# Mixing of the modes in a four-layer network: PE adds the two halves of each product with the identity, DVE sums the rest out of PSUM

## What is computed

```python
x_dht = jnp.fft.fftn(x.astype(jnp.complex64), axes=(2, 3)).real
top = jnp.einsum('bixy,ioxy->boxy', x_dht[:, :, :M1, :M2], weights1)
bot = jnp.einsum('bixy,ioxy->boxy', x_dht[:, :, -M1:, :M2], weights2)
...
y = jnp.fft.ifftn(out_dht.astype(jnp.complex64), axes=(2, 3)).real
```

## Time and profile before

| | |
|---|---|
| median of 3 runs | 3552.61 us (3551.06 to 3553.41) |
| profiled execution | 3554.87 us |
| its span in the trace | 3552.9 us |
| mean granted TensorE clock | 0.906 |
| PE / DVE / ACT / POOL busy | 76% / 79% / 47% / 51% of the span |

### The profile page before, as it was taken

The page is one execution under the profiler, slowest core; times in us unless marked ns, Lnnn a source line. Parts: engine busy times, 40 slices in busy tenths (PEclk is TensorE's granted clock), DMA queues, the critical chain, the costliest instruction groups (busy, mean ns, idle before and its releaser), DMA issues.

```text
span 3552.9 us, 48970 instructions
## 1 busy us (share of the span) xinstructions
PE 2697.3 (76%) x12701; PEld 2090.3 (59%) x12701; DVE 2797.8 (79%) x3703; ACT 1681.9 (47%) x2183; POOL 1816.0 (51%) x1292
## 2 busy tenths in 40 slices
PE   0094588699988439599989457869998853959998
PEld 0054467587746428487765446758774642848776
DVE  8985987688885888588878598768888588858887
ACT  7652145466643115556645214546664311555664
POOL 2003154399940237089990315439994023708998
PEclk9997889899999769799999788989999976979999
DMA  6712000888841100578880200088884110057885
GB/s 243 259 37 89 0 0 28 237 194 197 193 138 43 47 0 0 182 179 196 197 222 12 89 0 0 28 237 195 197 193 137 47 43 0 0 186 179 197 196 123
DMA packets 117444, 421.29 MB, mean 119 GB/s; under 512 B 16805, under 2 KB 30901, under 8 KB 106586
## 3 DMA queue, kind: packets, MB, share of 16 engines
q1 hardware_dynamic: 96390, 376.16, 41.1%
q10 hardware_dynamic: 19332, 38.99, 3.2%
q0 software_dynamic: 1616, 4.90, 0.5%
HBM read 340.43 MB, written 75.26 MB: 117 GB/s over the span
## 4 chain that ended last, share of the span: by engine, by line
PE 57%; DVE 18%; issue 14%; DMA 3%; POOL 3%; ACT 2%; DVEq 1%; ACTq 1%; SPq 0%; POOLq 0%
PE psum L536 25%; PE psum L503 15%; PE psum L412 7%; PE psum L438 3%; DVE img L1065 2%; POOL work L846 2%; PE psum L514 2%; PE psum L424 2%; DVE work L1044 2%; DVE small L886 2%; DVE work L1075 2%; DVE small L887 1%; DMA workr<-mx_dram 1%; DVE work L1058 1%; DVE work L1224 1%
## 5 line engine op out<-in xcount | busy, mean ns | idle before, releaser
L846 POOL TENSOR_TENSOR work<-work 128x512 f32<-128x512 f32 x960 | 1276.6, 1335 | 474.2 <-DVE work L1233 369.2
L536 PE MATMUL psum<-workr,w 128*128 128x512 f32 (+1 forms) x5760 | 1364.4, 397 | 122.3 <-DMA workr<-mx_dram 109.6
L536 PEld LDWEIGHTS psum<-workr,w 128*128 128x128 f32 (+1 forms) x5760 | 1088.8, 190 | 397.2 <-issue 110.5
L1224 DVE SCALAR_TENSOR_TENSOR work<-psum,work 128x512 f32<-128x512 f32 x1152 | 741.0, 679 | 69.5 <-PE psum L536 52.3
L824 POOL TENSOR_TENSOR work<-img 128x520 f32 x256 | 388.0, 1547 | 605.5 <-DVE img L1065 327.9
L503 PE MATMUL psum<-workr 128*128 128x512 f32 x2304 | 549.7, 401 | 43.5 <-DVE workr L1132 43.5
L503 PEld LDWEIGHTS psum<-workr 128*128 128x128 f32 x2304 | 438.7, 191 | 157.6 <-issue 48.3
L814 POOL TENSOR_TENSOR work<-work 128x1024 f32<-128x1024 f32 x40 | 112.5, 2841 | 503.3 <-DVE work L1033 498.9
L412 PE MATMUL psum<-work,taps 128*128 x1152 | 260.0, 389 | 53.9 <-DVE work L991 53.9
L696 ACT CAST workr<-psum 128x650 fp32r<-128x650 f32 x128 | 90.0, 703 | 445.6 <-DVE psum L1200 233.6
L1197 DVE TENSOR_TENSOR psum<-psum,work 128x650 f32<-128x650 f32 x128 | 107.9, 843 | 228.6 <-ACT psum L689 228.5
(11 more groups left out here) (184 smaller groups left out, 3519.2 us busy)
## 6 DMA issues: line engine op xcount, KB each, us to landing
work<-gn_dram SPq DMA_DIRECT2D x256, 585.0 KB, 11.5
work<-gn_dram SPq DMA_DIRECT2D x256, 146.2 KB, 3.8
work<-gn_dram SPq DMA_DIRECT2D x128, 292.5 KB, 4.8
work<-in_x SPq DMA_DIRECT2D x16, 2048.0 KB, 7.1
img<-in_x SPq DMA_DIRECT2D x32, 1024.0 KB, 11.7
work<-in_mixw SPq DMA_DIRECT2D x64, 512.0 KB, 4.2
out_x<-work ACTq DMA_DIRECT2D x120, 256.0 KB, 6.3
gn_dram<-img SPq DMA_DIRECT2D x24, 1040.0 KB, 21.2
```

What stands on the lines that cost most here:

```text
L536: mm = T.matmul(bank(m % 6), w5[wt][0:kr, P * n:P * n + P], ft[0:kr], start=(i == 0), stop=(i == 4))
L846: G.tensor_tensor(acc_t[v], acc_t[v], pd_t[(9 * v + n) % 6], ALU.add).then_inc(s_acc, 1)
L1224: V.scalar_tensor_tensor(out=tile4(pd_t[m % 6]), in0=tile4(psum[:, m % 6, :]), scalar=0.0, in1=rv[:, q, y0:y0 + RT, x0:x0 + WO], op0=ALU.m ...
```

## The change

PE gets a part in the mixing: for each product it multiplies the identity with the first 512 columns and with the last 512 and lets both add up in one bank of PSUM (banks 2 to 5, in turn). This sums input channels i and i + 16. `s_half16` counts these. DVE's reduction then reads 512 columns of PSUM, with 16 addends a sum, in place of 1024 of SBUF. PE waits for the product, for `spec` to be taken out of its banks (first two places), and from the fifth place on for the reduction four places back (`s_mix`).

The loop of two rounds on DVE is written out over 16 places, and DVE makes its own products up to three places ahead of the place that it reduces. SP issues the second load of a buffer after `s_half16`, not `s_mix`. POOL's program stays.

```diff
--- before.py
+++ after.py
@@ -229,7 +229,8 @@
         s_l1pe, s_l1act, s_l1dve = sem("s_l1pe"), sem("s_l1act"), sem("s_l1dve")
         s_row, s_rowps, s_spec = sem("s_row"), sem("s_rowps"), sem("s_spec")
         s_w = [sem(f"s_mixw{k}") for k in range(8)]
-        s_prodv, s_prod, s_mix, s_dup, s_ost, s_gz = sem("s_prodv"), sem("s_prod"), sem("s_mix"), sem("s_dup"), sem("s_ost"), sem("s_gz")
+        s_prodv, s_prod, s_half16, s_mix, s_dup, s_ost, s_gz = (sem("s_prodv"), sem("s_prod"), sem("s_half16"), sem("s_mix"),
+                                                                sem("s_dup"), sem("s_ost"), sem("s_gz"))
         s_inv, s_inva, s_invd, s_y1, s_x2 = sem("s_inv"), sem("s_inva"), sem("s_invd"), sem("s_y1"), sem("s_x2")
         s_pg, s_filt, s_fdiag, s_fsp, s_fbc, s_taps = (sem("s_pg"), sem("s_filt"), sem("s_fdiag"), sem("s_fsp"),
                                                        sem("s_fbc"), sem("s_taps"))
@@ -317,7 +318,7 @@
                         hold(sp, s_l1pe, b * L1PE + (NT + 10))
                     sp.dma_start(wr[k], mixw[:, 1024 * k:1024 * k + 1024]).then_inc(s_w[k], 16)
                 for n, k in enumerate(WR_DONE):
-                    hold(sp, s_mix, b * 16 + (n + 1))
+                    hold(sp, s_half16, b * 16 + (n + 1))
                     sp.dma_start(wr[k], mixw[:, 1024 * (8 + k):1024 * (9 + k)]).then_inc(s_w[k], 16)
 
                 sp.wait_ge(s_mix, b * 16 + 16)
@@ -454,6 +455,21 @@
                             mm = T.matmul(bank(2 + h), hc[:, m1, s, :], av[:, m1, 16 * h:16 * h + 16, s, :],
                                           start=(m1 + s == 0), stop=(m1 + s == 2))
                     mm.then_inc(s_l1pe, 1)
+
+                pooled = [k for k in range(8) if k not in WR_DVE]
+                for n in range(16):
+                    j, k = n // 8, WR_DONE[n % 8]
+                    if n >= 4:
+                        pe.wait_ge(s_mix, b * 16 + (n - 3))
+                    if n < 2:
+                        pe.wait_ge(s_spec, b + 1)
+                    if k in WR_DVE:
+                        pe.wait_ge(s_prodv, b * 6 + (3 * j + WR_DVE.index(k) + 1))
+                    else:
+                        pe.wait_ge(s_prod, b * 10 + (5 * j + pooled.index(k) + 1))
+                    for h in range(2):
+                        mm = T.matmul(bank(2 + n % 4), cs("ident"), wr[k][:, 512 * h:512 * h + 512], start=(h == 0), stop=(h == 1))
+                    mm.then_inc(s_half16, 1)
 
                 for g in range(16):
                     if g % 8 == 0:
@@ -1032,18 +1048,18 @@
                                          rrow[:, ch].unsqueeze(2).to_broadcast([P, 16, MODES]), ALU.mult))
                 V.tensor_tensor(sp3[:, :, 0], sp3[:, :, 0], rrow[:, C:2 * C], ALU.subtract).then_inc(s_spec, 1)
                 hold(v, s_spec, b + 1)
-                with v.Fori(0, 2) as j:
-                    pooled = [k for k in range(8) if k not in WR_DVE]
-                    for k in WR_DONE:
-                        if k in WR_DVE:
-                            v.wait_ge(s_w[k], b * 32 + j * 16 + 16)
-                            V.tensor_tensor(wr[k], wr[k], spec, ALU.mult).then_inc(s_prodv, 1)
-                            v.wait_ge(s_prodv, b * 6 + j * 3 + (WR_DVE.index(k) + 1))
-                        else:
-                            v.wait_ge(s_prod, b * 10 + j * 5 + (pooled.index(k) + 1))
-                        V.tensor_reduce(mixed[:, ds(j * (8 * MODES) + k * MODES, MODES)],
-                                        wr[k].rearrange("p (i l) -> p l i", l=MODES), AX.X, ALU.add
-                                        ).then_inc(s_mix, 1)
+                own = [(j, k) for j in range(2) for k in WR_DONE if k in WR_DVE]
+                made = 0
+                for n in range(16):
+                    while made < 6 and own[made][0] * 8 + WR_DONE.index(own[made][1]) <= n + 3:
+                        j, k = own[made]
+                        v.wait_ge(s_w[k], b * 32 + (16 * j + 16))
+                        V.tensor_tensor(wr[k], wr[k], spec, ALU.mult).then_inc(s_prodv, 1)
+                        made += 1
+                    v.wait_ge(s_half16, b * 16 + (n + 1))
+                    V.tensor_reduce(mixed[:, (n // 8) * (8 * MODES) + WR_DONE[n % 8] * MODES:][:, 0:MODES],
+                                    psum[:, 2 + n % 4, :].rearrange("p (i l) -> p l i", l=MODES), AX.X, ALU.add
+                                    ).then_inc(s_mix, 1)
                 v.wait_ge(s_dup, b * 64 + 64)
                 for h in range(2):
                     V.tensor_tensor(
```

## The result

The changed kernel takes 3526.24 us (median of 4 runs, 3524.67 to 3528.66) against 3553.01 for the kernel before (3551.06 to 3553.55): a ratio of 0.9926, 95% interval 0.9909 to 0.9943. The forecast was 3524.1: a gain of 28.5 us, of which 26.8 came. The profiled execution took 3526.67 us around a span of 3524.7; 3526.4 had been worked out for it. The mean granted clock rose from 0.906 to 0.927.

What follows compares the result with a forecast made beforehand. DVE was taken to bound each image's mixing stage; with PE summing, POOL and PE meet, PE's last place ends at 333.3 and the last reduction at 334.0, not 341.13: 7.1 us an image, 3552.61 - 28.5 = 3524.1 us, range 3513 to 3536.

Steps and rivals of the forecast that it cites:

- What bounds the stage: In the mixing, DVE sets the old end at 341.13 us; afterwards POOL's and PE's paths meet, at 331.3 and 331.4.
- The reduction: DVE's 16 new 128x512 reductions out of PSUM take 0.68 us each (0.94 at the upper end), the old ones 1.79.
- PE: In the mixing, two identity matmuls a product cost 1.72 us in a stream, 27.5 us for 16, hidden at full clock.
- POOL: Its ten mixing products, 2.34 us each plus six surcharges of 1.0, end at 331.1 us, without waiting for weights.
- DVE: Its mixing load becomes 10.9 us of reductions plus 9.4 us for six products, some 20 us; no longer the bound.
- The stage: The first image's mixing ends with the last reduction at 334.0 us, before at 341.13: a gain of 7.1 us.
- The passage to the span: Each microsecond taken from the mixing's end comes off the span, four times: 7.1 us an image, 28.5 in all.
- rival C: More gained: POOL hindered less, PE reaches L466 with clock up; up to 8 + 2 us an image, 3513 us; chance 0.07.
- A: PE bounds the mixing through low clock or more passes, 3.43 us a place: 17.8 us later, 3624 us; chance 0.05.
- B: Clock falls once in the mixing and returns, some 4.5 us at half; gain 5 us an image, 3533 us; chance 0.08.
- D: POOL takes the gain, all ten mixing products at 3.42 us: gain 2.2 us an image, 3544 us; chance 0.04.

Runs made afterwards that it cites:

- run 2: The changed kernel with one matmul a place on PE, the second half of each product left out of the sum: 3525.5 us.
- run 6: The changed kernel with DVE's six products cut from 1024 columns to 32, the rest left unmultiplied: 3520.0 us.
- run 3: The changed kernel with each place's two matmuls on PE issued twice: 3624.4 us.
- run 7: The changed kernel with a fourth piece (k = 3) given from POOL to DVE and the places in another order: 3525.6 us.
- run 8: The changed kernel with the edits of run 4 and run 7 together: 3524.0 us.
- run 10: The changed kernel with two added vector instructions of 1.2 us each an image, on the path behind the wait for the copies of mixed: 3539.7 us.
- run 4: The changed kernel plus eight identity matmuls into an unused bank behind the last place, filling PE's gap until the way back: 3523.3 us.

## Why the prediction was right

**What bounds the stage.** Right, and shown from both sides: less work on PE gives 1.2 us (run 2), on DVE and so on POOL 1.5 us (run 6), and twice the work on PE 25 us (run 3).

**The reduction.** 0.688 us [0.674 to 0.692], where 0.68 was taken and 0.94 was the other end. L1020's row was the one to go by: the new reduction with its step of 32 elements takes as long as L1188 (0.68 us). In SBUF it is another matter: the old reduction, with that step, took 1.87 us for 1024 columns, 1.83 ns a column, while a reduction of 4096 adjacent columns in the same trace (L886, a maximum) takes 4.41 us, 1.08 ns a column. The rows are the new reduction's in the changed kernel (ns min/median/max) and L886's (busy us, mean ns, idle time before):

```profile
L1060 DVE TENSOR_REDUCE work<-psum x64: 674/688/692, 311.0 to 2843.6; 128x32 f32<-128x512 f32 x64
...
L886 DVE TENSOR_REDUCE small<-work 128x4096 f32 x16 | 70.5, 4409 | 13.1 <-DMA work<-in_x 13.1
```

**PE.** 1.72 us a place was forecast, 1.75 came (with the last record's length in it); the full clock held, as rows 8 had let expect, with pauses of 2.4 us and less.

**POOL.** 28.84 us against 29.4: the surcharge of a DVE product is 0.91 us and not 1.0 (0.95 by run 6, where all six are gone). POOL never waited for weights in the first image, as worked out.

**DVE.** The term that was mis-sized: its six products take 13.2 us together, not the 9.4 of before (one of 3.37, one of 2.76); 23.5 us busy, not 20. The prediction had the rule in its sum, and used it for one product only: a DVE product that starts inside one of POOL's ends 1.1 us after it. The longest shows it, started at 318.96 and ended at 322.32, beside the two POOL products of that time:

```profile
318.90 2.34 POOL L830 TENSOR_TENSOR work<-work 128x1024 f32<-128x1024 f32 x1
321.20 3.33 POOL L830 TENSOR_TENSOR work<-work 128x1024 f32<-128x1024 f32 x1
```

Behind the fourth place PE waits no more for DVE's products, so this cost nothing.

**The stage.** 32.5 us, 32.9 forecast (334.0 - 301.12). A gain of 7.5 and not 7.1.

**The passage to the span.** This step was wrong as a rule, and that the sum came out all the same is luck. "A microsecond taken from 341.13 should be one taken from the span" holds for none of runs 2, 7, 8 and 10. In the change itself a gain of 7.5 us a stage became 9.1, 7.1 and 6.9 us in the three periods: the periods end at 836.2, two steps below 843.1 (843.1, 839.7, 836.2), and 7.5 us happened to lie near that. The prediction had the half-clock start at L466 as a thing of its own (rival C), with a price of 2 us; run 4 puts it at 2.9 us and shows that it is given back for the most part. The changed kernel pays more there than the one before: 6.0 us at half clock behind L482's start in the second image, against 4.7 us behind L466's start in the first image of before.

**The rivals.** A was priced rightly and didn't come. Nor did B: the granted clock is 1.00 over the whole stage. Of C came half a microsecond of POOL's surcharges (6 x 0.91 for 6 x 1.0), and the rest not: L482 starts at half clock as L466 did. D: POOL's unhindered product was 2.34 us as before while PE read the same buffers (2.31 in run 6), so PE's reads don't slow it.

## What to carry to other kernels

Moving part of an engine's work to an idle one pays only if the order feeds both: here the sum on PE without the look-ahead was 1.25% slower than no change, the look-ahead without PE 0.35% slower, both together 0.74% faster. Where PE enters stages at half clock, a time gained ahead of them isn't the time that arrives; it can shrink or grow on the way: look for the moment when the clock comes back, in both traces, before a small change is called useless. Filling PE's pauses with matmuls that nobody reads gave as much here as the change itself, and a shorter stage that had been worth nothing then counted.

## What the runs showed of the hardware

Not expected: in the kernels without filled pauses, with stages of 31 to 58 us, the second and third period of a run lie within 0.5 us of 833.0, 836.2, 839.7, 843.2, 846.5, 853.3 or 860.4 us, with one exception (836.9, run 2); the first is at times between (838.5, 838.7, 845.5, 852.1, 863.2). Of the run with filled pauses they are 829.7, 829.8 and 832.7 (with one long stage), of the last 828.9, 827.0 and 828.9: the steps are not gone for good, since the fills leave some pauses.

A DVE product of 128x1024 with both inputs in SBUF takes 1.22 us at the least. If it starts while one of POOL's runs, it ends 1.1 us after that one, whenever it began, so it takes up to 3.37 us in the changed kernel. One of POOL's takes 2.31 to 2.34 us, and 3.2 to 3.4 us if a DVE product is still under way when it starts or starts just ahead of it.
